# Two sub-blocks' products on ScalarE in walk steps 208 to 243 of a fused graph-attention and expert kernel

## What is computed

```python
xn = layernorm(x)
feat = (xn @ W).reshape(N, 4, 64)                 # graph attention, 4 heads
e = leaky_relu(el[src] + er[dst], 0.2)
alpha = softmax of e over the edges of each dst
msg = feat[src] * alpha[..., None]
rst = segment_sum(msg, dst)
x = x + (xn + elu(rst + bias)) + linear_attention(xn)
x = x + sum over top-2 of 8 experts of gate * (gelu(xe @ W1 + b1) @ W2 + b2)
```

## Time and profile before

| | us |
|---|---|
| median of 3 runs | 1897.31 |
| lowest, highest | 1894.27, 1901.55 |
| span of the profiled execution, first to last instruction | 1890.1 |
| the walk's first gather, about | 97 |
| slot 208 to slot 243 | 1031 to 1189 |
| last accumulate of the walk | 1198 |

### The profile page before, as it was taken

The page is one execution under the profiler, slowest core; times in us unless marked ns, Lnnn a source line. Parts: engine busy times, 40 slices in busy tenths (PEclk is TensorE's granted clock), DMA queues, the critical chain, the costliest instruction groups (busy, mean ns, idle before and its releaser), DMA issues. The chain is left out here.

```text
span 1890.1 us, 46784 instructions
## 1 busy us (share of the span) xinstructions
PE 1581.7 (84%) x11358; PEld 1300.0 (69%) x11358; DVE 1368.5 (72%) x3833; ACT 1079.1 (57%) x3043; POOL 1218.3 (64%) x1135
## 2 busy tenths in 40 slices
PE   7858777788787989888887778629999999999995
PEld 5635555455566777777775666517888889888884
DVE  6656567677667888888888999897666656665662
ACT  4655566566666666677666776563444444444441
POOL 2077777777777777777677776105666666666663
PEclk8978899999999999999998888658999999999998
DMA  7745565566544555555555665652333333333332
GB/s 223 247 122 138 168 174 164 165 176 179 150 117 127 155 150 150 141 152 145 142 139 179 183 202 162 200 199 45 53 48 53 49 48 50 53 50 49 46 53 24
DMA packets 149158, 239.37 MB, mean 127 GB/s; under 512 B 27536, under 2 KB 114824, under 8 KB 147624
## 3 DMA queue, kind: packets, MB, share of 16 engines
q0 software_dynamic: 61216, 132.39, 30.4%
q1 hardware_dynamic: 85944, 103.15, 16.8%
q10 hardware_dynamic: 1744, 0.85, 0.2%
HBM read 180.78 MB, written 55.52 MB: 125 GB/s over the span
## 5 line engine op out<-in xcount | busy, mean ns | idle before, releaser
L843 POOL DMA_INDIRECT w_s<-table,w_s x784 | 806.4, 1029 | 279.9 <-issue 231.4
L2092 PE MATMUL bank<-w_s 128*128 128x260 f32 x1952 | 515.9, 410 | 110.3 <-DVE w_s L1536 110.0
L2092 PEld LDWEIGHTS bank<-w_s 128*128 128x128 f32 x1952 | 378.1, 201 | 206.0 <-DVE w_s L1536 139.9
L1026 ACT ACTIVATE w_s<-w_s 128x64 f32 x976 | 260.3, 337 | 68.3 <-ACT w_s L1021 68.1
L1536 DVE SCALAR_TENSOR_TENSOR w_s<-w_s 128x256 f32<-128x256 f32 x732 | 275.7, 426 | 26.7 <-ACT w_s L1026 18.9
L2294 PE MATMUL bank<-acc,w_s 128*128 128x256 f16 (+1 forms) x2736 | 290.4, 265 | 1.6 <-DVE acc L1937 1.5
L2315 PE MATMUL bank<-w_s,acc 128*128 x2520 | 284.5, 273 | 7.2 <-DVE acc L1951 5.5
L907 POOL DMA_INDIRECT out<-mid_g,low_g x105 | 177.2, 1687 | 151.2 <-ACT mid_g L1197 90.6
L2294 PEld LDWEIGHTS bank<-acc,w_s 128*128 x2736 | 252.9, 98 | 30.7 <-issue 2.1
L2315 PEld LDWEIGHTS bank<-w_s,acc 128*128 128x128 f16 x2520 | 245.8, 98 | 37.0 <-issue 8.7
L1033 ACT COPY w_s<-bank 128x512 bf16<-128x512 bf16 x244 | 142.1, 582 | 202.8 <-PE bank L2072 202.3
(11 more groups left out here) (308 smaller groups left out, 2187.6 us busy)
## 6 DMA issues: line engine op xcount, KB each, us to landing
stage<-in_L_ffn_W SPq DMA_DIRECT2D x32, 512.0 KB, 4.2
w_s<-table,w_s POOLq DMA_INDIRECT x784
w_s<-in_x SPq DMA_DIRECT2D x48, 256.0 KB, 4.0
w_s<-xT_d SPq DMA_DIRECT2D x96, 128.0 KB
w_park<-low_g SPq DMA_DIRECT2D x18, 512.0 KB
w_s<-w_park SPq DMA_DIRECT2D x9, 1024.0 KB, 9.1
xn_d<-acc SPq DMA_DIRECT2D x7, 896.0 KB, 5.0
table<-w_s SPq DMA_DIRECT2D x24, 260.0 KB, 3.5
```

The costliest lines, as they stand in the source:

```text
L843: pool.indirect_dma_start(out=ring[:, u, k, :], out_offset=None, in_=table[:, :], in_offset=bass.IndirectOffsetOnAxis(ap=srcT[:, (q * RING ...
L1026: last = act.activation(m[:, e, 0:GD], rows[:, e, 0:GD], ACT.Copy, scale=m[:, e, GD:HC])
L2092: last = pe.matmul(bank[2 + k.at % 2][:, 0:ROW], hot32[:, k.at % 4, s, :], msg[:, k.at % 2, s, :], start=s == 0, stop=s == SUB - 1)
```

## The change

For steps from 208 on (`SHARED`), `own_of` is 2 and not 1: ScalarE makes the products of sub-blocks 2 and 3 (eight instructions), VectorE those of sub-blocks 0 and 1 (two), and VectorE's wait for `part_ready` stands before its second product. The fourth part of the logit of the next step stands ahead of the products in slots from 208 on. On GpSimd the value that each group's wait compares with is masked by a register instruction first. Lines of the changed kernel are 5 to 7 higher.

```diff
+SHARED = 208
...
+def own_of(k):
+    return 2 if k.past(SHARED) else 1
...
-                        pool.wait_ge(msg_ready, pool.snap(free_r[u], min_val=1, max_val=J))
+                        pool.wait_ge(msg_ready, pool.snap(pool.snap(free_r[u], min_val=1, max_val=J) & 255).with_bounds(min_val=1, max_val=J))
...
-                for e in range((SUB - 1) * GH, SUB * GH):
+                for e in range((SUB - own_of(k)) * GH, SUB * GH):
                     last = act.activation(m[:, e, 0:GD], rows[:, e, 0:GD], ACT.Copy, scale=m[:, e, GD:HC])
...
                 if scores:
                     dve_logit(j + 1, group1, slot1, 2)
+                if scores and own_of(j) == 2:
+                    dve_logit(j + 1, group1, slot1, 3)
                 if j.live():
                     dve_msg(j, dve.snap((last >> 8) & (RING - 1)).with_bounds(min_val=0, max_val=RING - 1))
                 if (j - 1).live() or not j.past(1):
                     load_step(j.n + 1, j.at + 1)
-                if scores:
+                if scores and own_of(j) == 1:
                     dve_logit(j + 1, group1, slot1, 3)
...
-                for e in range(0, (SUB - 1) * GH, GH):
-                    if e == (SUB - 2) * GH:
+                for e in range(0, (SUB - own_of(k)) * GH, GH):
+                    if e == (SUB - own_of(k) - 1) * GH:
                         dve.wait_ge(part_ready, k.n + 1)
```

## The result

| | before | changed |
|---|---|---|
| median of 5 runs, us | 1898.69 | 1911.46 |
| lowest, highest | 1894.27, 1901.55 | 1907.08, 1914.20 |
| span of the profiled execution | 1890.1 | 1905.4 |

The ratio is 1.0074, with a 95% interval of 1.0056 to 1.0092: slower by 0.7%, which is 14 us by the ratio and 12.8 us between the two medians. The forecast was 7 us slower, 1904.3, in a range of 1892 to 1913, with a chance of 0.31 for slower by more than 0.5%. Direction and place were right, the size was about half of what came.

A forecast was written before the change was run, and what follows sets the result against it. VectorE, 95% busy in the changed stretch, was taken as the bound. New waits of 17.7 us against 12.1 saved gave +5.6, plus 1.5 for TensorE's clock, minus 0.1: +7 us, 1904.3 us, range 1892 to 1913.

The forecast's parts named there:

- VectorE saves 0.34 us per step: From step 208 VectorE makes two products, not three: 0.337 us saved in each of 36 steps, 12.1 us.
- The last logit moves "at no cost by itself": VectorE's last logit instruction goes ahead of the products: no cost itself, products start 0.14 us later.
- bare slot: Slot where VectorE has only the step's own instructions, ten of them; predicted wait about 0.95 us behind each.
- The waits for ScalarE, stepped through at full clock: Slots 208 to 243: VectorE's waits for products 12.6, elu 5.0, split 4.4, together 22.0 us; 17.7 new.
- The term for TensorE's clock: Changed stretch: long sums at TensorE's low clock add +1.5 us, range 0 to +4.7.
- laden slots: Slots with extra VectorE work (1.1 us or more): wait 0, full 0.34 us won in most of 26.
- GpSimd's register instruction: One instruction ahead of each later gather group's wait on GpSimd: taken as hidden, 0 us.
- The walk's end gives back: Slot 243: GpSimd's add of a group covers a wait, giving back up to 0.7 us; forecast took -0.1.
- the sign of GpSimd's queue: If the walk reaches slot 100 later than before, GpSimd's queue is the cause.
- The 7.2 us "outside the span": Profiled span 1890.1 us lay 7.2 under the median 1897.31; the forecast added its 7 us to both.
- the one named third: Changed stretch: ScalarE and TensorE's low clock set the pace, +9.5 to +18, 1907 to 1915 us; chance 0.28.
- Rival 1: Changed stretch: ScalarE's part is in time, VectorE keeps all 12.1 us saved, 1885.2 us; chance 0.06.

The follow-up runs named there:

- order alone: Changed kernel with its new logit order, but three products on VectorE and four on ScalarE as before; ratios to the kernel before 0.9991 and 1.0029.
- work left out, old order: Changed kernel with sub-block 2's products made by nobody from step 208, last logit instruction behind the products; 1887.33 against 1895.70 us, ratio 0.9975.
- logit between: Changed kernel with the last logit instruction between VectorE's two products of a step; ratio 1.0075 to the kernel before.
- 23 steps: Changed kernel with logit between the two products, ScalarE making two sub-blocks only in 23 steps behind slots long on VectorE; ratio 1.0015 to the kernel before.
- the experiment on it: 16 spare TensorE matmuls added at ends of certain slots from 208, in changed kernel and kernel before (with register instruction); ratios 1.0103 and 1.0068.
- experiment 3: Kernel before with only the register instruction on GpSimd ahead of each group's wait; ratio 1.0015 to the kernel before.

## Why the prediction was right in direction and half in size

The stretch from the start of slot 208 to the start of slot 242 can be written as VectorE's busy time, its waits, and what is left in gaps too short to be listed:

| | stretch | busy | waits | short gaps |
|---|---|---|---|---|
| before | 154.8 | 148.1 | 5.7 | 1.0 |
| order alone | 160.0 | 153.1 | 3.0 | 3.9 |
| work left out, old order | 148.6 | 137.6 | 10.1 | 0.9 |
| logit between | 165.6 | 138.8 | 25.8 | 1.0 |
| changed kernel | 167.6 | 143.8 | 19.7 | 4.1 |
| 23 steps | 156.7 | 141.7 | 13.8 | 1.2 |

**VectorE saves 0.34 us per step: right.** 34 slots make 11.5 us; busy time fell by 10.5 with the work left out and by 9.3 with the logit between. Each new wait also ends an overlap of two rows and so adds 0.09 us to the busy time, 1.6 us for the 18 new ones with the logit between.

**The last logit moves "at no cost by itself": wrong.** It costs 0.27 us in a bare slot and about 8 us in all, shown by the order alone. I had looked at what the instruction costs at its old place and not at what stands ahead of it at the new one. But it isn't why the total was missed: with the logit between the products this cost is gone and the time is the same, as the waits take up its place.

**The waits for ScalarE, stepped through at full clock: place right, size short.** Up to slot 242 the 22.0 us predicted are 19.3. A wait listed in the trace is 0.09 us shorter than one of the stepping, since it counts from the end of the row before. With the logit between, the case that the prediction had worked out, the trace has 22.4 us in 29 waits, so 25.0: 5.7 more than stepped. In the changed kernel it has 18.2 in 27, so 20.6. Behind bare slots the prediction said 0.95 us with bare slots of 2.22. The changed kernel has 0.33 to 0.56 in slots 212, 217, 224 and 233, since its bare slots are 0.27 longer, and none in slot 238, but 1.05 to 1.29 in slots 229, 236 and 240.

**The term for TensorE's clock was mis-sized; this is the step that failed.** The stepping gave 4.7 us for the long sums, and I took 1.5, because it showed more waits on ScalarE in the kernel before than the trace. Up to slot 242 the stepping at full clock has 19.3 us of waits for ScalarE against 4.3 in the kernel before, 15.0 new ones, and 11.5 saved: a stretch 3.5 us longer. With the order free, as the prediction assumed it, it came out 10.8 us longer, 7.3 more. Of these 5.2 are waits for ScalarE (25.0 less 4.8 in the kernel before by the same count, in place of 15.0), 1.5 are VectorE's other waits, the rest is a slightly smaller saving. So what the stepping at full clock lacks in waits for ScalarE is 5.2 us, near the 4.7 that I had cut. The trace of the changed kernel shows how a long sum makes such a wait in slot 224 (1113.96 us). TensorE, ScalarE and VectorE:

```profile
1114.10 3.58 PE L2099 MATMUL bank<-w_s 128*128 128x260 f32 x8 [0.54 <-DVE w_s L1543]
...
1118.10 0.38 PE L2079 MATMUL bank<-w_s 128*128 128x128 bf16 x4
```
```profile
1118.52 0.58 ACT L1038 COPY w_s<-bank 128x512 bf16<-128x512 bf16 x1 [1.87 <-PE bank L2079]
...
1120.02 2.02 ACT L1031 ACTIVATE w_s<-w_s 128x64 f32 x8 [0.27 <-ACT w_s L1026]
```
```profile
1121.11 0.42 DVE L1543 SCALAR_TENSOR_TENSOR w_s<-w_s 128x256 f32<-128x256 f32 x1
1122.19 0.42 DVE L1543 SCALAR_TENSOR_TENSOR w_s<-w_s 128x256 f32<-128x256 f32 x1 [0.65 <-ACT w_s L1031]
```

The sum of step 223 takes 3.58 us and not 2.0, as in the earlier trace rows, at a granted clock of 0.59 from 1114 to 1118 us. So the one-hot of step 227 is turned at 1118.10, three microseconds after VectorE made it. ScalarE's copy starts 4.56 us into the slot and not 1.37, its eight products end at 1122.04, and VectorE waits 0.65 us although slot 224 was laden and 5.35 us long. With four products they would have ended at 1121.07, before VectorE needed them. The late copy is not new: in the kernel before it started 4.53 us into the same slot, behind a sum of 3.27 us, and with four products behind it VectorE waited 0.18 us. The prediction had these rows and still put the wait behind most laden slots at 0.

Four waits for the products in the changed kernel lie behind laden slots where the prediction had none: 0.63, 0.65, 1.03 and 1.05 us in slots 213, 225, 232 and 239, 3.4 us in sum. In each case a long sum (3.84, 3.58, 3.83 and 3.19 us, at a granted clock of 0.50 to 0.60) lies ahead of the turned one-hot that ScalarE waits for:

```profile
1054.11 3.84 PE L2099 MATMUL bank<-w_s 128*128 128x260 f32 x8 [0.51 <-DVE w_s L1543]
1149.58 3.83 PE L2099 MATMUL bank<-w_s 128*128 128x260 f32 x8 [0.47 <-DVE w_s L1543]
1184.86 3.19 PE L2099 MATMUL bank<-w_s 128*128 128x260 f32 x8 [0.89 <-DVE w_s L1543]
```

Beside the 2.0 us of the short ones each is long by more (1.2 to 1.8 us) than the wait that follows, and ScalarE stood idle before its copy for longer than that wait (0.91 to 2.67 us). So at full clock none of the four would be there; this is an estimate from the rows, not a test. Not every long sum makes a wait: of the changed kernel's 36 sums thirteen are longer than 2.3 us, against twelve before. The run with 23 steps has its largest waits in the same four slots. How much of the 5.2 us is the clock's in all was not shown; the experiment on it failed.

**GpSimd's register instruction: hidden**, as far as could be seen (experiment 3). **The walk's end gives back:** 2.3 us and not 0.1, most of it because the last sum fell into a stretch of full clock; the prediction had not looked for this, so it is luck. **Up to slot 208** nothing was changed but that instruction, and the changed kernel lags by 4.1 us there; the four kernels with the instruction on chip A lag by 2.2 to 4.8 us, in differing places. At slot 100 the changed kernel is 4.4 us late, which the prediction had named as the sign of GpSimd's queue. But the only profile of the kernel before is of an execution below its five times; this was not told apart from a small cost of the instruction. **The 7.2 us "outside the span"** were mostly this as well: the time lies 1.7 us above the span.

**The signs.** Of what the prediction would look for, the wait for the products came as said (10.9 us, 10 to 20 said). The elu's and the split's were 7.3 us and not 9, and slots 208 to 242 took 171.4 us (1035.3 to 1206.7) where 161 to 167 were said.

**Rivals.** By its time the case that came is the one named third (+9.5 to +18 us, the long sums cost the full amount), which had a chance of 0.28; that the long sums alone make the difference is not shown. Rival 1 was refuted by its own condition: VectorE waits 10.9 us for ScalarE's products, not under 5.

## What to carry to other kernels

A side engine with 30% idle time in the mean can still be unable to take work, if it can run ahead by one step only: compare its finishing time with the arrival of the bound engine slot by slot, with the slow instances of what it waits for put in where the trace has them. Work that is moved ahead of independent instructions, directly behind the instruction that it depends on, pays for the dependence: count the gap at the new place. When a stepping model gives the kernel before within 0.2 us, a correction to one of its terms for the kernel after needs a better reason than a mismatch in how its waits are named. And compare a profile's span with the times: both profiles here are of executions at or below the lowest time.

## What the runs showed of the hardware

Two small instructions on VectorE that depend on each other start 0.20 us apart, and the 128x256 product behind the second starts 0.29 us after it; in the old order it started 0.08 us behind the first (slot 223 in both kernels). A sum of eight 128x260 matmul rows took 2.0 us at a granted clock of 1.00 (1210.3 to 1212.4 us in the changed kernel) and 3.8 us at 0.50 (1149.6 to 1153.4 us). Chips differ: the same kernel took 1896 us on one and 2275 and 2307 us on two others. On the first of these two VectorE's instructions are as long (its product 420 ns in experiment 3's run, 421 in the kernel before); what is longer is its waits.
